# Convolutional linear attention and softmax attention in one kernel: tap copies on two queues, key taps between token products, and a last layer that works on pairs of images

## The chip, the cores and the metric

The kernel runs on one core of one Trainium2 chip. The metric is device time in microseconds (us), the median of several executions. TensorE multiplies, ScalarE and VectorE evacuate PSUM and do element-wise work, GpSimd does element-wise work in SBUF, and SyncE issues transfers; GpSimd and ScalarE issue some too.

## The reference

The input x is 4 images of 128 channels and 16 x 16 pixels, float32. The first layer is multi-scale linear attention:

```python
qkv = _conv(x, w_qkv)                      # 1x1, 384 channels
agg = _conv(_conv(qkv, w_dw, groups=384, pad=2), w_pw, groups=48)
qkv = concat([qkv, agg], axis=1)           # 32 heads of 24 channels: q, k, v of 8
q, k = relu(q), relu(k); v = pad(v, ones)
vk = einsum('bhdn,bhen->bhde', v, k)
out = einsum('bhde,bhen->bhdn', vk, q)
x = x + _conv(out[:, :, :-1] / (out[:, :, -1:] + EPS), w_proj)
```

The second layer is softmax attention over the 256 pixels of each image, with two 64-channel projections:

```python
t, p = W_theta @ x + b_theta, W_phi @ x + b_phi      # 64 x 256 per image
f = softmax(einsum('ndq,ndk->nqk', t, p) / 8, axis=-1)
x = x + W_fuse @ einsum('nqk,nck->ncq', f, x) + b_fuse
```

## The kernel before, in words

Every engine has a program written out by hand, in order; semaphores join them. There is no scheduler and no planner, so the order of the code is the order of the work.

**Opening.** SyncE loads the weights, then the depthwise 5 x 5 taps into tap_base (4 transfers, L303). The convolution works on pixels split into four phases, so a tap table shifted by a phase is needed on 128 partitions. For K this is done by TensorE: key_taps (L665) multiplies tap_base by a selection matrix. For Q and V it is done by transfers: SyncE waits for the taps and copies tap_base to tap_all sixteen times, 8 partitions each, for 4 phases and 4 quads (L316, semaphore taps_copied). VectorE's kept_taps (L491) multiplies taps by a mask, six operations for each kind, into wsel; wsel times the pointwise weights wpw_t gives wconv, by VectorE for K (L514) and by GpSimd for Q and V (L350, L355).

**Tokens, planes, convolution.** by_pixel (L671) makes the tokens of K, Q or V for one pair of images: four products, evacuated by ScalarE for pair 0 and by ScalarE or VectorE for pair 1 (L378, L475). to_planes (L682) transposes them, in the order pair 0, pair 1, pair 0, pair 1 in each half; ScalarE and VectorE copy these planes (L382, L479). convolve (L691) runs 144 products of 32 x 32 tiles for each kind, in three or four pieces with other work between them. The convolution of Q waits for wconv of Q, for the planes of Q, and for both evacuations of the convolution of K (L386, L532). Ahead of it stand plain_queries (L699) and some transposes of weights.

**Middle.** Key sums, denominators (L719), value-key products (L729), reciprocals and projections follow, all with TensorE as the engine that sets the pace.

**Last layer.** project(b, 1) (L859) finishes the first layer for image b in bank FIRST[b]; VectorE's first_layer (L606) adds xs into x1. Then for each image theta_phi_values makes in one bank, SECOND[b], the 128 rows of theta and phi (L885, 256 columns) and the values times W_fuse (L887, twice 128 columns). ScalarE evacuates theta and phi apart, 64 partitions each (L432, L434), into halves of tiles that hold two images. scores(pair) (L896) needs thetas and phis of both images of the pair, and uses each half of the array's rows for one image. VectorE takes the maxima (L610), ScalarE the exponentials with their sums (L445, two for each image), VectorE normalizes (L620, L623), TensorE transposes (L908), ScalarE evacuates for images 0, 2 and 3 (L451) and VectorE for image 1 (L627). attend (L916) gives the result, and VectorE adds bias and x1 (L633), which SyncE stores.

The order of the last layer is a list of steps for each engine; TensorE's is

```python
for step, b in ((theta_phi_values, 0), (theta_phi_values, 1), (theta_phi_values, 2), (scores, 0),
                (theta_phi_values, 3), (scores, 1), (transpose_probs, 0),
                (transpose_probs, 1), (attend, 0), (transpose_probs, 2), (attend, 1),
                (transpose_probs, 3), (attend, 2), (attend, 3)):
```

## Time and profile before

| what | value |
|---|---|
| median of 3 runs | 75.73 us (75.58 to 78.31) |
| the profiled execution | 75.22 us |
| its span, first to last instruction | 73.4 us |
| busy in the span: PE, VectorE, ScalarE, GpSimd | 63.9, 37.9, 24.5, 16.2 us |
| granted TensorE clock, mean | 1.00 |
| last ys written, end of the span | 71.3, 73.4 us |

Times of the trace are counted from the start of the span. The span lacks 1.8 us of the profiled execution's time. PE is TensorE's matmuls and PEld its weight loads; a float32 product appears as two records, a transpose as one. An idle time is put down to what ended it, in square brackets.

### The profile page before, as it was taken

How to read it: one execution, taken by the hardware profiler on the slowest of the kernel's cores; microseconds unless marked ns; L12 is line 12 of the kernel's file. 1: busy time of each engine (PE TensorE's matmuls, PEld its weight loads, DVE VectorE, ACT ScalarE, POOL GpSimd, SP SyncE). 2: the span in 40 equal slices, each digit the busy share in tenths (PEclk: the TensorE clock that was granted, in tenths of full speed). 3: DMA queues.
4: the chain of work that ended last, by engine and by line, in shares of the span. 5: the costliest groups of instructions: out<-in, count | busy, mean ns of one | idle time of the engine just before them, and what ended most of it. 6: DMA issues, size and time to landing. Idle time of an engine off the chain costs nothing.

```text
span 73.4 us, 2866 instructions
## 1 busy us (share of the span) xinstructions
PE 63.9 (87%) x1297; PEld 46.0 (63%) x1297; DVE 37.9 (52%) x96; ACT 24.5 (33%) x57; POOL 16.2 (22%) x22
## 2 busy tenths in 40 slices
PE   3999958999999699999999999999899591839960
PEld 3669846777867267466655766569589470628750
DVE  4540193002998547435049079595383037299660
ACT  0742460020317403005303000550203949688500
POOL 4307910000779999700000000000000000000000
PEclk9999999999999999999999999999999999999999
DMA  0863400002100000000000000000000000000143
GB/s 0 268 129 108 116 17 16 20 16 54 29 9 9 0 0 9 0 9 0 13 0 9 0 9 0 9 0 0 0 0 9 0 0 0 4 0 0 50 136 101
DMA packets 3484, 2.11 MB, mean 29 GB/s; under 512 B 1360, under 2 KB 3424, under 8 KB 3472
## 3 DMA queue, kind: packets, MB, share of 16 engines
q1 hardware_dynamic: 2672, 1.19, 6.0%
q10 hardware_dynamic: 544, 0.52, 2.1%
q0 software_dynamic: 256, 0.21, 1.2%
q8 instruction: 10, 0.16, 0.9%
q14 instruction: 2, 0.02, 0.1%
HBM read 1.24 MB, written 0.52 MB: 24 GB/s over the span
## 4 chain that ended last, share of the span: by engine, by line
PE 51%; SPq 15%; DVE 14%; DMA 7%; ACT 6%; issue 3%; ACTq 0%
PE bank L691 18%; SPq L316 13%; PE bank L916 5%; DMA tap_base<-in_L_conv_w_dw 4%; PE bank L859 4%; DVE wsel L491 4%; PE bank L896 3%; PE bank L739 3%; PE bank L729 3%; PE bank L705 3%; DMA tap_all<-tap_base 3%; PE bank L831 2%; PE bank L908 2%; ACT phi L434 2%; ACT theta L432 2%
## 5 line engine op out<-in xcount | busy, mean ns | idle before, releaser
L691 PE MATMUL bank<-planes,wconv 32*32 32x256 f32 x864 | 19.9, 397 | 1.7 <-DVE wconv L514 1.0
L691 PEld LDWEIGHTS bank<-planes,wconv 32*32 32x32 f32 x864 | 11.6, 103 | 8.3 <-issue 3.4
L671 PEld LDWEIGHTS bank<-wqkv_t,xp 128*128 128x128 f32 x48 | 6.5, 216 | 1.1 <-issue 0.9
L671 PE MATMUL bank<-wqkv_t,xp 128*128 128x128 f32 x48 | 6.8, 302 | 0.0
L491 DVE TENSOR_TENSOR wsel<-tap_all,consts 128x24 f32<-128x24 f32 x12 | 3.1, 327 | 6.3 <-DMA tap_all<-tap_base 6.3
L610 DVE TENSOR_REDUCE nmx<-bank 128x2 f32<-128x512 f32 x4 | 2.7, 687 | 5.5 <-PE bank L896 5.5
L378 ACT ACTIVATE toks<-bank 128x512 f32<-128x512 f32 x4 | 2.4, 597 | 9.0 <-PE bank L671 9.0
L649 PE MATMUL bank<-warm 128*128 128x256 f32 x8 | 4.0, 654 | 1.2 <-DVE warm L460 1.2
L896 PE MATMUL bank<-phi,theta 64*128 64x256 f32 x16 | 2.3, 402 | 2.5 <-ACT phi L434 2.5
L859 PE MATMUL bank<-qs,m 128*128 128x256 f32 x16 | 4.4, 402 | 0.0
L386 ACT ACTIVATE conv<-bank 128x512 f32<-128x512 f32 x3 | 1.8, 598 | 7.8 <-PE bank L691 7.8
L445 ACT ACTIVATE pr<-bank,nmx 128x256 f32<-128x256 f32 x8 | 3.7, 475 | 1.9 <-DVE nmx L610 1.8
L916 PE MATMUL bank<-pt,gf 128*128 128x256 f32 (+1 forms) x20 | 4.3, 352 | 0.0
L350 POOL TENSOR_TENSOR wconv<-wsel,wpw_t 128x1152 f32<-128x1152 f32 x1 | 2.2, 2175 | 9.3 <-DVE wsel L491 9.3
L554 DVE TENSOR_TENSOR vk<-bank,consts 64x128 f32<-64x128 f32 x8 | 2.3, 289 | 3.0 <-PE bank L729 2.9
L382 ACT ACTIVATE planes<-bank 128x512 f32<-128x512 f32 x4 | 2.4, 640 | 4.1 <-PE bank L682 4.1
L908 PE MATMUL bank<-ident,pn 128*128 128x128 f32 x16 | 2.5, 279 | 1.2 <-DVE pn L623 1.2
L562 DVE RECIPROCAL rden<-den 128x256 f32<-128x256 f32 x2 | 3.5, 1754 | 0.1
L649 PEld LDWEIGHTS bank<-warm 128*128 128x128 f32 x8 | 2.4, 333 | 1.5 <-DVE warm L460 1.2
L916 PEld LDWEIGHTS bank<-pt,gf 128*128 128x128 f32 x20 | 3.0, 190 | 0.6 <-ACT pt L451 0.2
L896 PEld LDWEIGHTS bank<-phi,theta 64*128 64x128 f32 x16 | 1.4, 186 | 3.0 <-ACT phi L434 2.9
L859 PEld LDWEIGHTS bank<-qs,m 128*128 128x128 f32 x16 | 2.7, 189 | 0.8 <-DVE qs L566 0.3
(107 smaller groups left out, 102.8 us busy)
## 6 DMA issues: line engine op xcount, KB each, us to landing
xs<-in_x ACTq DMA_DIRECT2D x2, 256.0 KB, 3.4
out<-ys SPq DMA_DIRECT2D x3, 128.0 KB, 1.7
tap_all<-tap_base SPq DMA_DIRECT2D x16, 9.6 KB
wqkv_n<-in_L_conv_w_qkv SPq DMA_DIRECT2D x3, 64.0 KB, 2.8
consts<-in_shape_constants POOLq DMA_DIRECT2D x1, 184.0 KB, 2.7
wproj_n<-in_L_conv_w_proj SPq DMA_DIRECT2D x1, 128.0 KB, 2.3
out<-ys SPq DMA_DIRECT2D x2, 64.0 KB, 1.6
tap_base<-in_L_conv_w_dw SPq DMA_DIRECT2D x4, 9.4 KB
```

The costliest lines, as they stand in the source:

```text
L316: sp.dma_start(dst, src).then_inc(taps_copied, 16)
L445: nc.scalar.activation(pr[:, b, qc, :], bank[:, FIRST[b], qc * N:(qc + 1) * N], ACT.Exp, bias=nmx[:, b, qc:qc + 1], accum_out=rs[:, b, qc: ...
L491: last = nc.vector.tensor_tensor(sel, src, mask, ALU.mult)
L562: nc.vector.reciprocal(rden[a][:, :], den[a][:, :]).then_inc(rden_out[a], 1)
L610: nc.vector.tensor_reduce(nmx[:, b, :], bank[:, FIRST[b], :].rearrange("p (q n) -> p q n", q=2), AX_X, ALU.max, negate=True).then_inc(nmx_ ...
L649: nc.tensor.matmul(bank[:, WARM, 0:N], warm[:, 0:P], warm[:, :], start=True, stop=True)
L671: last = nc.tensor.matmul(bank[:, TOK[kind][pair], a * P:(a + 1) * P], xp[:, pair, a, :], wqkv_t[:, kind, :], start=True, stop=True)
L691: last = nc.tensor.matmul(bank[32 * quad:32 * (quad + 1), i, 0:NPIX], w, window(i, kind, quad, n // WIN, n % WIN), start=n == 0, stop=n == ...
L859: last = nc.tensor.matmul(bank[:, FIRST[b], 0:N], m2[a][:, b, :], qs[:, b, a, :], start=a == 0, stop=a == 1)
L896: last = nc.tensor.matmul(bank[:, FIRST[2 * pair + n], qc * N:(qc + 1) * N], theta[rows, pair, qc * P:(qc + 1) * P], phi[rows, pair, :], s ...
L908: last = nc.tensor.transpose(bank[:, SECOND[b], at:at + P], pn[:, b, qc, kc * P:(kc + 1) * P], ident[:, :])
L916: last = nc.tensor.matmul(dst, gf[:, b, kc, :], pt[:, b, kc, pixels], start=kc == 0, stop=kc == 1)
```

## The change

**Tap copies.** SyncE issues those of phases 0 and 1, GpSimd those of phases 2 and 3, behind wpw_r and ahead of its constants and biases, with waits of its own for tap_base. VectorE waits for both semaphores ahead of wsel of Q and of V.

**Key taps.** TensorE does key_taps between the two token products of K, no longer behind them.

**Last layer.** thetas_phis(pair) makes the theta of both images of a pair in one bank, image 0 in the array's lower and image 1 in its upper 64 columns, and phi in another. ScalarE evacuates theta of a pair in one instruction of 128 partitions, VectorE phi in one. The values of a pair come later, together in one bank (the one that theta of the pair had), and are evacuated by one instruction of 512 columns on ScalarE. ScalarE evacuates all four images' transposed probabilities. The orders of all three engines are new. The step thetas_phis(0) stands ahead of project(3, 1).

```diff
+        THETA, PHI, GF, PT, REST = (2, 0), (3, 1), (2, 0), (3, 1, 2, 0), 3
...
+        def shifted_taps(a, i):
+
+            shift = TAPS * (a // 2) + a % 2
+            return (tap_all[32 * i + E * a:32 * i + E * (a + 1), :],
+                    tap_base[E * i:E * (i + 1), shift:shift + TAP_LEN + TAP_PAD])
...
-            for a in range(PHASES):
-                shift = TAPS * (a // 2) + a % 2
+            for a in range(PHASES // 2):
                 for i in range(QUADS):
-                    src = tap_base[E * i:E * (i + 1), shift:shift + TAP_LEN + TAP_PAD]
-                    dst = tap_all[32 * i + E * a:32 * i + E * (a + 1), :]
-                    sp.dma_start(dst, src).then_inc(taps_copied, 16)
+                    sp.dma_start(*shifted_taps(a, i)).then_inc(taps_copied, 16)
...
+            pool.wait_ge(base_zero, 2)
+            pool.wait_ge(ld_taps, 16 * QUADS)
+            for a in range(PHASES // 2, PHASES):
+                for i in range(QUADS):
+                    pool.dma_start(*shifted_taps(a, i)).then_inc(taps_moved, 16)
...
+            def thetas(pair):
+                act.wait_ge(theta_mm, pair + 1)
+                nc.scalar.activation(theta[:, pair, :], bank[:, THETA[pair], 0:N], ACT.Identity, bias=bth_s[:, 0:1],
+                                     scale=D ** -0.5).then_inc(theta_out, 1)
+
+            def values(pair):
+                act.wait_ge(gf_mm, pair + 1)
+                nc.scalar.activation(gf[:, 2 * pair:2 * pair + 2].rearrange("p b k c -> p (b k c)"), bank[:, GF[pair], :],
+                                     ACT.Copy).then_inc(gf_out, 1)
...
-                    dve.wait_ge(taps_copied, 16 * PHASES * QUADS)
+                    dve.wait_ge(taps_copied, 8 * PHASES * QUADS)
+                    dve.wait_ge(taps_moved, 8 * PHASES * QUADS)
...
+            def phis(pair):
+                dve.wait_ge(phi_mm, pair + 1)
+                nc.vector.tensor_scalar_add(phi[:, pair, :], bank[:, PHI[pair], 0:N], bph[:, 0:1]).then_inc(phi_out, 1)
...
+            for step, n in ((first_layer, 0), (first_layer, 1), (first_layer, 2), (phis, 0), (first_layer, 3), (maxima, 0),
+                            (phis, 1), (maxima, 1), (normalize, 0), (maxima, 2), (normalize, 1), (maxima, 3),
+                            (normalize, 2), (normalize, 3), (result, 0), (result, 1), (result, 2), (result, 3)):
+                step(n)
...
             by_pixel(K, 0)
-            pe.wait_ge(xp_act[1], 1)
-            pe.wait_ge(xp_dve[1], 1)
-            by_pixel(K, 1)
             pe.wait_ge(sel_set, 1)
             pe.wait_ge(base_zero, 2)
             pe.wait_ge(ld_taps, 16 * QUADS)
             key_taps()
+            pe.wait_ge(xp_act[1], 1)
+            pe.wait_ge(xp_dve[1], 1)
+            by_pixel(K, 1)
...
+            def thetas_phis(pair):
+
+                pe.wait_ge(x1_out, 2 * pair + 2)
+                for cols, i, done in ((slice(0, D), THETA[pair], theta_mm), (slice(D, 2 * D), PHI[pair], phi_mm)):
+                    for n in range(2):
+                        last = nc.tensor.matmul(bank[D * n:D * (n + 1), i, 0:N], wtp_t[:, cols], x1[:, 2 * pair + n, :],
+                                                start=True, stop=True)
+                    last.then_inc(done, 1)
+
+            def values(pair):
+                pe.wait_ge(theta_out, pair + 1)
+                for n in range(2):
+                    for kc in range(2):
+                        at = n * N + kc * C
+                        last = nc.tensor.matmul(bank[:, GF[pair], at:at + C], x1[:, 2 * pair + n, kc * P:(kc + 1) * P],
+                                                wfuse_t[:, :], start=True, stop=True)
+                last.then_inc(gf_mm, 1)
 
             def scores(pair):
-                pe.wait_ge(tp_out, 4 * pair + 4)
+                pe.wait_ge(theta_out, pair + 1)
+                pe.wait_ge(phi_out, pair + 1)
...
-                pe.wait_ge(gf_out[b], 1)
+                if b >= 2:
+                    pe.wait_ge(gf_out, b - 1)
...
-                pe.wait_ge(pt_out[b], 1)
+                pe.wait_ge(pt_out, b + 1)
+                pe.wait_ge(gf_out, b // 2 + 1)
...
+            project(2, 1)
+            thetas_phis(0)
+            project(3, 1)
+            scores(0)
+            thetas_phis(1)
+            values(0)
+            scores(1)
+            values(1)
+            transpose_probs(0)
+            transpose_probs(1)
+            attend(0)
+            transpose_probs(2)
+            attend(1)
+            transpose_probs(3)
+            attend(2)
+            attend(3)
 
```

TensorE in the opening, where xp are the pixels of x, tap_base the taps and toks the tokens; before:

```order
L671 MATMUL bank<-wqkv_t,xp 128x128 x8
L665 MATMUL bank<-tap_base,tap_sel 128x124 x4
L768 MATMUL bank<-ident,wpw_r 128x96
L682 MATMUL bank<-ident,toks 128x128 x8
L657 MATMUL bank<-ident,wqkv_n 128x128 x2
```

and of the change:

```order
L672 MATMUL bank<-wqkv_t,xp 128x128 x4
L666 MATMUL bank<-tap_base,tap_sel 128x124 x4
L672 MATMUL bank<-wqkv_t,xp 128x128 x4
L769 MATMUL bank<-ident,wpw_r 128x96
L683 MATMUL bank<-ident,toks 128x128 x8
```

The four products of taps (L665, now L666) stand four products earlier, and the second pair of K's tokens behind them.

TensorE at the start of the last layer, from the projections (qs, m) on; before:

```order
L859 MATMUL bank<-qs,m 128x256 x4
L885 MATMUL bank<-x,wtp_t 128x256
L887 MATMUL bank<-wfuse_t,x 128x128 x2
L885 MATMUL bank<-x,wtp_t 128x256
L887 MATMUL bank<-wfuse_t,x 128x128 x2
L885 MATMUL bank<-x,wtp_t 128x256
L887 MATMUL bank<-wfuse_t,x 128x128 x2
L896 MATMUL bank<-phi,theta 128x256 x4
L885 MATMUL bank<-x,wtp_t 128x256
L887 MATMUL bank<-wfuse_t,x 128x128 x2
L896 MATMUL bank<-phi,theta 128x256 x4
```

and of the change:

```order
L860 MATMUL bank<-qs,m 128x256 x3
L882 MATMUL bank<-x,wtp_t 64x256 x4
L860 MATMUL bank<-qs,m 128x256
L901 MATMUL bank<-phi,theta 128x256 x4
L882 MATMUL bank<-x,wtp_t 64x256 x4
L891 MATMUL bank<-wfuse_t,x 128x128 x4
L901 MATMUL bank<-phi,theta 128x256 x4
L891 MATMUL bank<-wfuse_t,x 128x128 x4
```

The products of x1 with wtp_t (theta and phi) are now of 64 columns and stand ahead of a projection and behind the first scores (phi, theta); those with wfuse_t (values) stand behind or between the scores.

ScalarE from the first theta on; before:

```order
L432 ACTIVATE theta<-bank,bth_s 64x256
L434 ACTIVATE phi<-bank,bph 64x256
L439 ACTIVATE gf<-bank 128x256
L432 ACTIVATE theta<-bank,bth_s 64x256
L434 ACTIVATE phi<-bank,bph 64x256
L432 ACTIVATE theta<-bank,bth_s 64x256
L434 ACTIVATE phi<-bank,bph 64x256
L445 ACTIVATE pr,rs<-bank,nmx 128x256 x2
L432 ACTIVATE theta<-bank,bth_s 64x256
L434 ACTIVATE phi<-bank,bph 64x256
L445 ACTIVATE pr,rs<-bank,nmx 128x256 x4
L451 ACTIVATE pt<-bank 128x512
```

and of the change:

```order
L440 ACTIVATE theta<-bank,bth_s 128x256 x2
L451 ACTIVATE pr,rs<-bank,nmx 128x256 x2
L445 ACTIVATE gf<-bank 128x512
L451 ACTIVATE pr,rs<-bank,nmx 128x256 x2
L445 ACTIVATE gf<-bank 128x512
L451 ACTIVATE pr,rs<-bank,nmx 128x256 x2
L457 ACTIVATE pt<-bank 128x512
L451 ACTIVATE pr,rs<-bank,nmx 128x256 x2
L457 ACTIVATE pt<-bank 128x512 x3
```

Phi is gone from ScalarE, each remaining theta and gf is of a pair, and four of pt stand there where there were three.

## Rows read from the trace of the kernel before

**Rows 1.** The page, chain that ended last, shares of the span by line

```profile
PE bank L691 18%; SPq L316 13%; PE bank L916 5%; DMA tap_base<-in_L_conv_w_dw 4%; PE bank L859 4%; DVE wsel L491 4%; PE bank L896 3%; PE bank L739 3%; PE bank L729 3%; PE bank L705 3%; DMA tap_all<-tap_base 3%; PE bank L831 2%; PE bank L908 2%; ACT phi L434 2%; ACT theta L432 2%
```

**Rows 2.** Tile tap_all: duration in ns min/median/max, first and last start

```profile
L316 SPq DMA_DIRECT2D tap_all<-tap_base x16: 624/625/753, 5.9 to 16.1; - x16
L491 DVE TENSOR_TENSOR wsel<-tap_all,consts x12: 172/175/1858, 17.9 to 21.4; 128x24 f32<-128x24 f32 x12
```

**Rows 3.** Chain in order of time: start, us, what

```profile
16.08 1.84 DMA tap_all<-tap_base
```

**Rows 4.** Timeline, opening: start, us, engine, line, operation, count, idle before

```profile
5.10 2.74 PE L671 MATMUL bank<-wqkv_t,xp 128*128 128x128 f32 x16
...
6.29 0.55 POOL L341 DMA_DIRECT2D consts<-in_shape_constants  x1
...
6.98 0.60 ACT L378 ACTIVATE toks<-bank 128x512 f32<-128x512 f32 x1 [1.44 <-PE bank L671]
...
7.76 1.15 PE L665 MATMUL bank<-tap_base,tap_sel 32*128 32x124 f32 x8
...
7.87 0.60 ACT L378 ACTIVATE toks<-bank 128x512 f32<-128x512 f32 x1 [0.29 <-PE bank L671]
...
8.99 1.04 PE L682 MATMUL bank<-ident,toks 128*128 128x128 f32 x8
...
9.69 1.16 ACT L382 ACTIVATE planes<-bank 128x512 f32<-128x512 f32 x2 [1.23 <-PE bank L682]
...
9.85 1.36 DVE L514 TENSOR_TENSOR wconv<-wsel,wpw_t 128x1152 f32<-128x1152 f32 x1
...
11.26 2.20 PE L691 MATMUL bank<-planes,wconv 32*32 32x256 f32 x96 [1.02 <-DVE wconv L514]
```

**Rows 5.** The page, transfers: KB each, median us from issue to landing

```profile
bth<-in_L_conv_b_theta POOLq DMA_DIRECT2D x2, 0.2 KB, 2.2
```

**Rows 6.** Timeline, 17 to 26 us, ahead of the convolution of Q

```profile
17.51 2.05 PE L671 MATMUL bank<-wqkv_t,xp 128*128 128x128 f32 x16
...
18.76 2.17 POOL L350 TENSOR_TENSOR wconv<-wsel,wpw_t 128x1152 f32<-128x1152 f32 x1 [9.31 <-DVE wsel L491]
...
22.18 1.41 DVE L527 MEMSET vk<- 64x256 f32 x4
...
23.24 1.13 PE L699 MATMUL bank<-xs,wqkv_t 128*128 128x512 f32 x2
...
23.63 0.69 DVE L532 TENSOR_SCALAR conv<-bank 128x512 f32<-128x512 f32 x1
...
25.06 2.20 PE L691 MATMUL bank<-planes,wconv 32*32 32x256 f32 x96 [0.70 <-DVE planes L479]
```

**Rows 7.** Timeline, denominators (L719) and the last layer

```profile
36.94 0.64 PE L719 MATMUL bank<-rq,ks 128*32 128x256 f32 x8
...
53.99 1.72 DVE L606 TENSOR_TENSOR x<-bank,xs 128x256 f32<-128x256 f32 x4
...
56.25 0.47 ACT L432 ACTIVATE theta<-bank,bth_s 64x256 f32<-64x256 f32 x1 [3.04 <-PE bank L887]
...
58.66 1.13 PE L896 MATMUL bank<-phi,theta 64*128 64x256 f32 x8 [0.78 <-ACT phi L434]
...
59.73 0.70 PE L885 MATMUL bank<-x,wtp_t 128*128 128x256 f32 x2
...
62.61 1.13 PE L896 MATMUL bank<-phi,theta 64*128 64x256 f32 x8 [1.75 <-ACT phi L434]
...
64.50 0.47 ACT L445 ACTIVATE pr<-bank,nmx 128x256 f32<-128x256 f32 x1 [0.90 <-DVE nmx L610]
...
65.42 0.60 ACT L451 ACTIVATE pt<-bank 128x512 f32<-128x512 f32 x1
...
67.50 1.13 PE L916 MATMUL bank<-pt,gf 128*128 128x256 f32 x4
...
69.97 1.33 DVE L633 SCALAR_TENSOR_TENSOR ys<-bank,bfu,x 128x256 f32<-128x256 f32 x3 [0.82 <-PE bank L916]
```

**Rows 8.** Busy us of each engine from 60 to 66, granted clock, transfers

```profile
60.00:66.00 6.00, 3.01 (x22) 2.15 (x21) 4.08 (x11) 4.47 (x16) 0.00 (x0) 1.00 0.00 1
```

More of the change, by code:

```diff
@@ L426, in _ @@
             act.wait_ge(bias_scaled, 1)
-            def theta_phi(b):
-                act.wait_ge(tf_mm, b + 1)
-                src = bank[:, SECOND[b], :]
-                rows = slice(D * (b % 2), D * (b % 2 + 1))
-                nc.scalar.activation(theta[rows, b // 2, :], src[0:D, 0:N], ACT.Identity, bias=bth_s[rows, 0:1],
-                                     scale=D ** -0.5).then_inc(tp_out, 1)
-                nc.scalar.activation(phi[rows, b // 2, :], src[D:2 * D, 0:N], ACT.Identity,
-                                     bias=bph[rows, 0:1]).then_inc(tp_out, 1)
-            def values(b):
-                act.wait_ge(tf_mm, b + 1)
-                nc.scalar.activation(gf[:, b].rearrange("p k c -> p (k c)"), bank[:, SECOND[b], N:2 * N],
-                                     ACT.Copy).then_inc(gf_out[b], 1)
+            def thetas(pair):
[6 more added lines that the diff above has]
+                                     ACT.Copy).then_inc(gf_out, 1)
             def exponentials(b):
@@ L450, in transposed @@
                 act.wait_ge(pt_mm, b + 1)
-                nc.scalar.activation(pt[:, b].rearrange("p k n -> p (k n)"), bank[:, SECOND[b], :], ACT.Copy).then_inc(pt_out[b], 1)
-            for step, b in ((theta_phi, 0), (values, 0), (theta_phi, 1), (theta_phi, 2), (exponentials, 0),
-                            (theta_phi, 3), (exponentials, 1), (exponentials, 2), (transposed, 0), (values, 2),
-                            (exponentials, 3), (values, 3), (transposed, 2), (transposed, 3)):
-                step(b)
+                nc.scalar.activation(pt[:, b].rearrange("p k n -> p (k n)"), bank[:, PT[b], :], ACT.Copy).then_inc(pt_out, 1)
+            for step, n in ((thetas, 0), (thetas, 1), (exponentials, 0), (values, 0), (exponentials, 1), (values, 1),
+                            (exponentials, 2), (transposed, 0), (exponentials, 3), (transposed, 1), (transposed, 2),
+                            (transposed, 3)):
+                step(n)
         @block.vector
@@ L637, in _ @@
             nc.vector.tensor_scalar_mul(bth_s[:, :], bth[:, :], D ** -0.5).then_inc(bias_scaled, 1)
[L638 to L642 removed]
+            for step, n in ((first_layer, 0), (first_layer, 1), (first_layer, 2), (phis, 0), (first_layer, 3), (maxima, 0),
+                            (phis, 1), (maxima, 1), (normalize, 0), (maxima, 2), (normalize, 1), (maxima, 3),
+                            (normalize, 2), (normalize, 3), (result, 0), (result, 1), (result, 2), (result, 3)):
+                step(n)
         @block.tensor
@@ L917, in attend @@
                     last.then_inc(y_mm, 1)
-            for step, b in ((theta_phi_values, 0), (theta_phi_values, 1), (theta_phi_values, 2), (scores, 0),
-                            (theta_phi_values, 3), (scores, 1), (transpose_probs, 0),
-                            (transpose_probs, 1), (attend, 0), (transpose_probs, 2), (attend, 1),
-                            (transpose_probs, 3), (attend, 2), (attend, 3)):
-                step(b)
+            pe.wait_ge(m2_act[1], 1)
+            project(0, 1)
+            project(1, 1)
+            pe.wait_ge(m2_dve, 1)
+            project(2, 1)
[14 more added lines that the diff above has]
+            attend(3)
 _INS = ["x", "L0_conv_w_qkv", "L0_conv_w_dw", "L0_conv_w_pw", "L0_conv_w_proj", "L1_conv_W_theta",
```

40 lines of the change are left out of this document (8 added, 32 removed).

## The prediction

> **What bounds the kernel now.** I read the chain that ended last by line first, then the chain in order of time, then the timeline of its two weak places, the opening and the last layer. The chain is mostly TensorE, but its second largest line is no work at all: SyncE's issues of the tap copies, 13% [rows 1]. The reader is to see sixteen issues of 0.62 us one behind the other, first start 5.9, last start 16.1 [rows 2], and behind them a landing of 1.84 us that ends at 17.92 [rows 3]. Only then, at 17.9, can VectorE make wsel of Q [rows 2]. The share of 13% is not what can be won, though: TensorE works on through all of this, and what it loses is read from its own idle time, 0.70 us ahead of the convolution of Q at 25.06 [rows 6]. So the tap copies are worth 0.7 us, not 10. Nearly everything between 25 and 53 us is TensorE without a pause, and I move it as one block. The third place is the last layer: there TensorE stands idle twice ahead of the scores (L896), 0.78 and 1.75 us, each time for a phi that ScalarE evacuates [rows 7]. Between 60 and 66 us it is busy for only 3.01 of 6 us [rows 8]. That is the large loss.
>
> **Key taps between the token products.** TensorE does not wait for anything up to 7.8 us, so only the order changes. Sixteen records of L671 take 2.74 us from 5.10, and the clock they run at is lower in the first half: ScalarE could start on pair 0 at 6.98 and on pair 1 at 7.87 [rows 4]. The taps (1.15 us) come at about 6.9 and are done at 8.0, 0.9 us earlier than before (7.76 + 1.15 = 8.91). VectorE's wsel of K goes with them, but what follows it, wpw_t, waits for a transpose that TensorE issues at 8.85 as before; I let wpw_t start at 9.2, behind that transpose; its quarter of a microsecond brings wconv of K to 9.5 instead of 9.85, so that its 1.36 ends about 0.35 earlier, near 10.85 [rows 4]. Against that, the second pair of K's tokens is now done at 8.8 instead of 7.85. ScalarE's 0.60 for it ends at 9.4, and the transposes to planes, which from the second one on need both pairs, cannot go before. Before, planes started 0.70 behind the first transpose (8.99 to 9.69); now three of the four transposes of that half are left at 9.45, 2 steps of 0.11 and 0.27 to the end of the last, and planes start at 9.98. Its 1.16 ends at 11.1, and the first convolution starts at 11.2 instead of 11.26. I take 0.05 gained, so nothing: the wait for wconv has become a wait for planes. The bounds are 0.35 gained (planes not late) and 0.75 lost, which is next.
>
> **Taps on two queues.** SyncE issues 8 instead of 16 copies: 5.89 + 8 x 0.66 = 11.2, and with 1.84 they land at 13.0 [rows 2, 3]. GpSimd issues the other 8 from 6.33 (behind wpw_r, and its new waits for tap_base, which landed at 5.8). No row shows a GpSimd issue of this shape; the nearest are 0.55 for a large constant and 2.2 us of landing for a small bias [rows 4, 5]: 6.33 + 8 x 0.55 + 2.2 = 12.9. So both halves are there at 13.0, 4.9 us sooner. Behind them on GpSimd's queue stand the constants and five bias loads, each moved by 4.4 us, to about 13.9, then wconv of Q. The constants are wanted at 33, the biases at 54. SyncE's three last-layer weights are issued 5.3 us earlier and nobody waits for them.
>
> What VectorE makes of it: wsel of Q runs at 13.0 to 13.7, the Q tokens as TensorE delivers them near 15.5, wsel of V directly after, the V tokens at 19.6 (TensorE's 17.51 + 2.05), the zero fills (1.41) until about 21.7 [rows 6]. At 21.7 the convolution of K is done, and its evacuation starts at once instead of at 23.63; the Q planes are ready by 23.5. TensorE's last work ahead of the convolution of Q, plain_queries, ends at 24.37 (23.24 + 1.13). It starts there: **0.70 us gained**, and not more, since TensorE's own work ends last. GpSimd's wconv of Q (2.17) is done at about 16.1, long before. One stall goes with it and gives nothing more: one of the twelve wsel operations took 1.86 us where the median is 0.175 [rows 2], beside GpSimd's wconv of 18.76 to 20.9 [rows 6]. Now wsel of V starts only when that wconv is over.
>
> That row is also the danger. It reads as if VectorE's first wsel of V was held until GpSimd's multiplication was over, so that the two exclude each other for some operations. The Trainium skill (SBUF — State Buffer, "SBUF: two separate sides") says that VectorE in some modes and GpSimd share a port pair by an exclusive lock, and that the descriptors of GpSimd's DMAs are written through it. The trace agrees for the multiplication, by the 1.86 us; for DMA issues no row shows it. In this kernel it would be wconv of K on VectorE, at 9.5, beside the last two issues of taps and those of the constants. At worst the two issues that are left at 9.5 hold it, 2 x 0.55 = 1.1 us; 0.35 of that is cover, so 0.75 lost at the first convolution, and the 0.70 is gone. I take zero: what held VectorE was a multiplication over whole tiles, and a DMA issue is not that.
>
> **The last layer.** I lay it out in the times of before, to be moved by 0.70 as a whole. Removed: eight evacuations of 64 partitions by ScalarE (0.47 each, 3.8 us), replaced by two thetas on ScalarE and two phis on VectorE. Four values of 256 columns become two of 512. All four transposed probabilities now go to ScalarE, which loses VectorE's help there (0.6 more). Step by step [rows 7]:
> - x1 of image 1 is there at 53.99 + 2 x 0.43 = 54.85. The theta and phi products of the pair use 64 columns of the array each. No row has that tile. The nearest are L719, four tiles of 32 columns, whose 8 records take 0.64 us, that is side by side, and L896, two tiles of 64 rows, 8 records in 1.13. If they don't overlap, 8 records cost 8 x 0.22 = 1.7 instead of 0.9. I take L896's 1.13: phi is ready at 56.0, VectorE's 0.43 ends at 56.45, scores start at 56.5 (before: 58.66).
> - Projection 3 is tucked between; x1 of image 3 comes at 56.9 instead of 55.7, still ahead of its use.
> - TensorE is free 1.07 after the scores start (58.66 to 59.73): 57.6 [rows 7]. Then theta and phi of pair 1 (0.96), values 0 (eight records of 0.11 and 0.1 for the switch, 1.0), scores 1 (1.0), values 1 (its results 1.15 after its start): 58.55, 59.55, 60.5, 61.65. Without a wait, since theta 1 is ready at 58.8, phi 1 at 59.1.
> - ScalarE: exponentials 0 and 1 fit before 61.65. From there on: values 1 0.60, exponentials 2 0.92 (64.50 to 65.42), transposed 0 0.60, exponentials 3 0.92, transposed 1 0.60, with 0.05 at the seams: 65.4. Attend 1 starts there, before it was at 67.50. TensorE has done attend 0 and the transposes of image 2 meanwhile (63.9 to 65.2).
> - From attend 1 to the end the work is the same: 67.50 to the end of the last ys, 71.30, is 3.80. Image 3's probabilities are normalized at 65.7, transposed at 66.3. **2.1 us gained.**
>
> Each switch between whole array and halves costs 0.1 in my sum: four rounds of L896, 0.22 apart (two records of L885 take 0.70, one 0.48), are 0.88, and the next product came after 1.07; I give half of the 0.19 to the start behind a wait and half to the switch. I have six switches on the path. The Trainium skill (TensorEngine Tiling (Array Packing), "Tiling Modes", Key Properties) says that changing the mode drains TensorE. By a full drain L885 could not have started before L896's last end, 59.79, where it started at 59.73: 0.06 more for each switch, 0.4 for six, and 1.7 gained in place of 2.1. The row decides for me.
>
> **Sum.** 0.70 + 2.1 = 2.8 off the profiled execution's 75.22: 72.4. The median of the runs, 75.73, lies 0.5 above that execution; but I counted every evacuation of ScalarE at its full length, with no overlap at the seams. I say 72.5.
>
> **Rivals.**
> 1. The 64-column products don't overlap. Then 0.87 more twice, 1.7: 74.2. For it: no row has the tile. Against it: L719.
> 2. The opening gives nothing, because GpSimd's issues hold VectorE's wconv of K: 75.22 - 2.1 = 73.1, or 73.2 with the offset. For it: the 2.47 row. Against: its cover of 0.35.
> 3. ScalarE binds the last layer. From theta 1 (58.3) to transposed 1 it has nine steps: 0.47 + 4 x 0.92 + 4 x 0.60 = 6.55, to 64.9, which is 0.5 short of binding. If exponentials take 1.05 and each step pays 0.1 at its seam, that is 66.3 and attend 1 is 0.9 late: 73.3, and 73.7 with full drains. For it: it inherits all four transposed probabilities. Against it: it loses half of its theta and phi work.
> 4. Slower: the clock falls in the last layer. Up to 6.8 us L671's records came at 0.215, later products of that size at 0.11, so half speed doubles them. If it fell behind the scores 0, the chain would hold 4.1 us (57.6 to 61.65) and 3.1 (attend 1 to the end) of TensorE's work: 72.4 + 7.2 = 79.6. It decides from 2.8 us of such work on the chain (4.3 for slower by 2%). Against it: the granted clock stayed at 1.00 between 60 and 66 us with pauses up to 1.75 [rows 8], and the longest new pause in my layout is 1.4, ahead of attend 0.
>
> **Chances.** Forecast 0.62 (its own range 71.3 to 73.3); rival 1 0.10; rival 2 0.11; rival 3 0.07; rivals 1 and 2 together, 74.9, 0.07; rival 4 0.03. About 2% is what a measurement of this kernel can tell from no change, so faster means under 74.2. The forecast, rivals 2 and 3 and half of rival 1 are under it: 0.85; the rest of 1, and 1 with 2, is the same: 0.12; slower 0.03. Range 71.3 (planes not late, switches free: 0.35 and 0.5 more) to 74.2.
>
> **What would show it.** Right: no issue of taps in the chain; wsel of Q near 13; the convolution of Q 0.7 us earlier, without an idle wait; theta and phi records in pairs with the same start; scores near 55.8 and attend 1 near 64.7. Wrong: wconv of K on VectorE over 1.4 us; records of L882 spread 0.22 apart without pairs; ScalarE waiting over 0.5 us ahead of an exponential; a last granted clock under 1.00.

## The result, and the profile after

The changed kernel takes 72.53 us (median of 4 runs, 72.38 to 72.72); the kernel before, run beside it, takes 76.87 (median of 4, 75.58 to 78.31). Runs in a slower state, like the 78.00 and 78.31 of the kernel before, are left out of all ratios. The ratio is 0.963, interval 0.960 to 0.966. The forecast was 72.5 in a range of 71.3 to 74.2. The profiled execution took 72.72 for the 75.22 of before, its span 70.6 for 73.4: 2.8 us less in the span and 2.5 in all. In two profiles below the granted clock is 0.50 for a while (both opening edits alone, from 62.7 to 69.5 us, and the new last layer alone, from 25.5 to 28.9), and only their other stages are read.

The page of the changed kernel, the chain that ended last by engine and by line; it answers to [rows 1]:

```profile
PE 86%; ACT 5%; DVE 4%; issue 1%; ACTq 0%
PE bank L692 27%; PE bank L672 9%; PE bank L923 6%; PE bank L650 5%; PE bank L683 4%; PE bank L860 3%; PE bank L740 3%; PE bank L730 3%; PE bank L901 3%; PE bank L891 3%; PE bank L700 3%; PE bank L882 3%; PE bank L706 3%; PE bank L832 2%; DVE vk L561 2%; ACT planes L392 2%
```

SyncE's issues, 13% before, are gone from the chain. What took their place is TensorE's own work in the opening (L672, L683, the warm-up products L650), which had been there all the time beside them. That is why 13% of the chain were worth only 1% of the time.

The timeline of the changed kernel's opening, columns as in [rows 4]; it answers to [rows 4] and [rows 6]:

```profile
5.18 1.26 PE L672 MATMUL bank<-wqkv_t,xp 128*128 128x128 f32 x8
6.03 5.47 SPq L321 DMA_DIRECT2D tap_all<-tap_base  x8
6.37 1.15 PE L666 MATMUL bank<-tap_base,tap_sel 32*128 32x124 f32 x8
6.76 4.05 POOL L350 DMA_DIRECT2D tap_all<-tap_base  x8 [0.28 <-issue]
7.45 1.16 PE L672 MATMUL bank<-wqkv_t,xp 128*128 128x128 f32 x8
8.65 0.60 ACT L388 ACTIVATE toks<-bank 128x512 f32<-128x512 f32 x1 [1.57 <-PE bank L672]
9.10 1.36 DVE L521 TENSOR_TENSOR wconv<-wsel,wpw_t 128x1152 f32<-128x1152 f32 x1
9.30 0.98 PE L683 MATMUL bank<-ident,toks 128*128 128x128 f32 x7 [0.49 <-ACT toks L388]
9.95 1.16 ACT L392 ACTIVATE planes<-bank 128x512 f32<-128x512 f32 x2 [0.70 <-PE bank L683]
11.25 2.20 PE L692 MATMUL bank<-planes,wconv 32*32 32x256 f32 x96 [0.75 <-ACT planes L392]
...
13.61 0.65 DVE L498 TENSOR_TENSOR wsel<-tap_all,consts 128x24 f32<-128x24 f32 x6 [2.58 <-DMA tap_all<-tap_base]
14.43 2.17 POOL L360 TENSOR_TENSOR wconv<-wsel,wpw_t 128x1152 f32<-128x1152 f32 x1 [0.43 <-DVE wsel L498]
...
16.14 1.10 DVE L498 TENSOR_TENSOR wsel<-tap_all,consts 128x24 f32<-128x24 f32 x6
...
24.28 1.70 PEld L692 LDWEIGHTS bank<-planes,wconv 32*32 32x32 f32 x96 [0.76 <-issue]
24.28 2.10 PE L692 MATMUL bank<-planes,wconv 32*32 32x256 f32 x90
```

The reader is to see: the taps arrive at 13.6 instead of 17.9; the convolution of Q starts at 24.28 instead of 25.06 and PE waits for no engine ahead of it; the first convolution starts where it did (11.25 for 11.26), but what ended its wait is now the planes, not wconv, which was ready at 10.46. And the first eight records of token products take 1.26 us, where the sixteen of [rows 4] took 2.74: the clock rose earlier in this execution. That will matter below.

The last layer of the changed kernel; it answers to [rows 7]:

```profile
54.11 1.08 PE L882 MATMUL bank<-x,wtp_t 128*64 128x256 f32 x8
54.89 0.47 ACT L440 ACTIVATE theta<-bank,bth_s 128x256 f32<-128x256 f32 x1 [2.48 <-PE bank L882]
55.12 0.30 PEld L860 LDWEIGHTS bank<-qs,m 128*128 128x128 f32 x2 [0.39 <-issue]
55.12 0.70 PE L860 MATMUL bank<-qs,m 128*128 128x256 f32 x2
55.24 0.48 DVE L622 TENSOR_SCALAR phi<-bank,bph 128x256 f32<-128x256 f32 x1 [0.75 <-PE bank L882]
...
55.87 1.14 PE L901 MATMUL bank<-phi,theta 64*128 64x256 f32 x8
...
61.30 0.60 ACT L445 ACTIVATE gf<-bank 128x512 f32<-128x512 f32 x1 [0.64 <-PE bank L891]
...
61.79 0.47 ACT L451 ACTIVATE pr<-bank,nmx 128x256 f32<-128x256 f32 x1
...
62.69 0.60 ACT L457 ACTIVATE pt<-bank 128x512 f32<-128x512 f32 x1
...
63.17 0.49 ACT L451 ACTIVATE pr<-bank,nmx 128x256 f32<-128x256 f32 x1
...
63.35 1.13 PE L923 MATMUL bank<-pt,gf 128*128 128x256 f32 x4 [1.02 <-ACT pt L457]
...
64.75 1.13 PE L923 MATMUL bank<-pt,gf 128*128 128x256 f32 x4
...
67.22 1.33 DVE L635 SCALAR_TENSOR_TENSOR ys<-bank,bfu,x 128x256 f32<-128x256 f32 x3 [0.82 <-PE bank L923]
```

Attend 1 starts at 64.75 for 67.50 before, and the last ys ends at 68.55 for 71.30: 2.75 us, of which 0.78 came in with the convolution of Q. The stretch of 60 to 66 us, to be held against [rows 8]:

```profile
60.00:66.00 6.00, 4.98 (x33) 4.05 (x32) 4.01 (x13) 4.66 (x16) 0.00 (x0) 1.00 0.00 0
```

TensorE is busy for 4.98 of the 6 us where it was for 3.01, at the same granted clock.

### The profile page after: what moved, and what is told of

It is laid out like the page before. It is cut to its first block, busy times and chain, and to the rows that moved or that the text cites. A ratio compares the mean times of both kernels' runs of the same rounds, so it can differ in the third digit from the quotient of the medians.

```text
span 70.6 us, 2883 instructions
## 1 busy us (share of the span) xinstructions
PE 64.2 (91%) x1305; PEld 44.8 (63%) x1305; DVE 37.0 (52%) x96; ACT 22.1 (31%) x51; POOL 20.4 (29%) x30
## 4 chain that ended last, share of the span: by engine, by line
PE 86%; ACT 5%; DVE 4%; issue 1%; ACTq 0%
PE bank L692 27%; PE bank L672 9%; PE bank L923 6%; PE bank L650 5%; PE bank L683 4%; PE bank L860 3%; PE bank L740 3%; PE bank L730 3%; PE bank L901 3%; PE bank L891 3%; PE bank L700 3%; PE bank L882 3%; PE bank L706 3%; PE bank L832 2%; DVE vk L561 2%; ACT planes L392 2%
## 5 line engine op out<-in xcount | busy, mean ns | idle before, releaser
L672 PEld LDWEIGHTS bank<-wqkv_t,xp 128*128 128x128 f32 x48 | 6.0, 199 | 1.2 <-issue 0.9
L672 PE MATMUL bank<-wqkv_t,xp 128*128 128x128 f32 x48 | 6.5, 287 | 0.0
L650 PE MATMUL bank<-warm 128*128 128x256 f32 x8 | 4.0, 654 | 1.2 <-DVE warm L466 1.2
L350 POOL DMA_DIRECT2D tap_all<-tap_base x8 | 4.1, 514 | 0.3 <-issue 0.3
L683 PE MATMUL bank<-ident,toks 128*128 128x128 f32 x24 | 3.4, 280 | 0.5 <-ACT toks L388 0.5
L683 PEld LDWEIGHTS bank<-ident,toks 128*128 128x128 f32 x24 | 2.6, 141 | 1.6 <-issue 0.9
L650 PEld LDWEIGHTS bank<-warm 128*128 128x128 f32 x8 | 2.4, 333 | 1.5 <-DVE warm L466 1.2
L481 DVE COPY toks<-bank 128x512 f32<-128x512 f32 x2 | 1.4, 692 | 3.6 <-PE bank L672 3.6
L485 DVE COPY planes<-bank 128x512 f32<-128x512 f32 x2 | 1.4, 692 | 3.3 <-PE bank L683 3.3
```

Of the source, the lines that this page charges most:

```text
L350: pool.dma_start(*shifted_taps(a, i)).then_inc(taps_moved, 16)
L650: nc.tensor.matmul(bank[:, WARM, 0:N], warm[:, 0:P], warm[:, :], start=True, stop=True)
L672: last = nc.tensor.matmul(bank[:, TOK[kind][pair], a * P:(a + 1) * P], xp[:, pair, a, :], wqkv_t[:, kind, :], start=True, stop=True)
L683: last = nc.tensor.transpose(bank[:, PLANE[kind][half], n * P:(n + 1) * P], src, ident[:, :])
```

## The experiments

Eleven kernels were run and the changed one a second time. Since medians of one kernel differ by more than some of the parts (last experiment), I read each part from its stage in the profile, and give the ratio to the kernel before beside it. All the stage lengths are differences of starts in the timelines:

| kernel | slow steps | first token product to first convolution | first convolution to that of Q | last projections to last ys | ratio to before (interval) |
|---|---|---|---|---|---|
| before | 8 | 6.16 | 13.80 | 18.04 | |
| changed | 2 | 6.07 | 13.03 | 16.09 | 0.963 (0.960 to 0.966) |
| tap copies on two queues alone | 0 | 5.38 | 13.04 | 18.04 | 0.983 (0.977 to 0.990) |
| key taps moved alone | 1 | 6.20 | 14.26 | 18.04 | 0.999 (0.996 to 1.003) |
| both opening edits | 1 | 5.97 | 13.10 | (clock) | none |
| last layer alone | 0 | 5.38 | 14.81 | 16.08 | 0.974 (0.968 to 0.980) |
| same half | 0 | 5.96 | 13.04 | 17.79 | none |
| projection first | 0 | 6.01 | 13.04 | 16.37 | 0.974 (0.968 to 0.980) |
| values later | 4 | 6.31 | 13.04 | 15.21 | 0.956 (0.949 to 0.964) |
| VectorE helps | 1 | 5.95 | 13.05 | 15.99 | 0.970 (0.959 to 0.981) |
| key taps in old place | 7 | 6.05 | 13.04 | 16.09 | 0.959 (0.952 to 0.965) |
| best | 2 | 5.56 | 13.03 | 15.21 | 0.954 (0.950 to 0.958) |
| taps last on GpSimd | 7 | 6.86 | 13.03 | 16.09 | 0.971 (0.968 to 0.973) |
| changed, again | 4 | 6.27 | 13.03 | 16.08 | 0.970 (0.965 to 0.974) |

"Slow steps" counts, of the sixteen records of K's first token products, those that follow the one ahead by more than 0.16 us (most of them by 0.21) and not by 0.11. I take them for the time that the clock stayed at its lower level (1.2 of 2.4 GHz). The profile's clock column reads 1.00 in this stretch too, but the trace's first entry of a full clock stands at 6.7 us in the kernel before and at 5.6 in the changed one, where the steps become short; and from 66 to 69 us of the profile of both opening edits, where the granted clock is 0.50, records of 128 columns come at the same 0.21. One step of 0.21 is not counted: the second record behind the taps has it in every kernel with the new order, also at 7.67 us of the changed one, long after the clock has risen. "Last projections" is the first product of project(0, 1).

**Tap copies on two queues alone.** The edit is the part of the change on SyncE, GpSimd and VectorE's wait, in the kernel before.

> The kernel before, with only the tap copies on two queues. My theory: TensorE's idle time of 0.70 us ahead of the convolution of Q goes, and nothing else in the opening counts: 0.7 to 0.8 us less than the kernel before, near 74.8 by medians. The rival, that the opening's gain needs the key taps' new place too (the first convolution earlier), gives less than 0.4. The rival that GpSimd's issues hold VectorE's wconv of K shows wconv of K over 1.4 us and gives nothing.

```profile
10.41 2.20 PE L700 MATMUL bank<-planes,wconv 32*32 32x256 f32 x96 [1.02 <-DVE wconv L523]
...
23.45 2.20 PE L700 MATMUL bank<-planes,wconv 32*32 32x256 f32 x96
```

Its timeline: the convolution of Q comes 13.04 after the first, for 13.80 before, and its own idle note is gone: 0.76 us, all of the idle time and no more. The first convolution is early too, at 10.41; the edit has no part in that, since its reason is the 0 slow steps, and the new last layer alone, whose opening is that of before, has 0 slow steps and the same 5.38. GpSimd's issues did not hold wconv of K. My theory holds for the stage, and its number. By time the kernel is 1.3 us below the one before (74.20 for 75.51 by medians), more than I expected; in the profile the early first convolution is 0.85 of it.

**Key taps moved alone.**

```diff
             by_pixel(K, 0)
-            pe.wait_ge(xp_act[1], 1)
-            pe.wait_ge(xp_dve[1], 1)
-            by_pixel(K, 1)
...
             key_taps()
+            pe.wait_ge(xp_act[1], 1)
+            pe.wait_ge(xp_dve[1], 1)
+            by_pixel(K, 1)
```

> The kernel before, with only the key taps moved between the two token products of K. My theory: wconv of K is ready 0.35 us earlier, but the planes of K come later than it, so the first convolution starts within 0.15 of 11.26 and the time is the same within 0.2 us. The rival, that the planes are not late, starts it at 10.9; then TensorE waits longer ahead of the convolution of Q instead, since the tap copies still land at 17.9, and the time is the same as well, so the start of the first convolution tells them apart, not the time.

Its timeline, TensorE in the opening:

```profile
4.77 1.16 PE L671 MATMUL bank<-wqkv_t,xp 128*128 128x128 f32 x8
6.13 1.12 PE L665 MATMUL bank<-tap_base,tap_sel 32*128 32x124 f32 x8 [0.20 <-DMA tap_base<-in_L_conv_w_dw]
7.18 1.16 PE L671 MATMUL bank<-wqkv_t,xp 128*128 128x128 f32 x8
...
9.03 0.98 PE L682 MATMUL bank<-ident,toks 128*128 128x128 f32 x7 [0.49 <-ACT toks L378]
...
10.97 0.84 PE L691 MATMUL bank<-planes,wconv 32*32 32x256 f32 x33 [0.75 <-ACT planes L382]
```

The time is the same, as both theories said, because the taps of Q still land late: the 14.26 us to the convolution of Q swallow whatever happens ahead. The start of the first convolution, 10.97, is nearer to the rival's 10.9 than to mine. But the comparison with 11.26 was wrong, for both: that number belongs to a profile with 8 slow steps, this one has 1. Counted from the first token product, the old order takes 5.38 with no slow step and 5.56 with 2 (best, below), and this one takes 6.20. So it is neither theory: the move costs time. The rows say how. The first convolution waits for planes, the planes for the transposes, these for the second pair of tokens, and that now stands behind 1.1 us of taps and, when the clock is early, behind a wait of 0.20 for tap_base as well.

**Both opening edits, old last layer.**

> The kernel before, with both edits of the opening and the old last layer. My theory: 0.75 us less than before, the same as the tap copies on two queues alone within 0.15. The rival, that the two edits help each other: 1.0 us or more less than before.

No ratio can be given: its four runs took 74.10 to 76.84 us, two of them at a mean granted clock of 0.955 and 0.954. Its opening gives 13.10 to the convolution of Q and 5.97 to the first: what the two edits do alone, and no help of one to the other that the rival wanted. Inconclusive as to time.

**Last layer alone.** The changed kernel with both opening edits undone.

> The changed kernel with both edits of the opening undone. My theory: the parts add up, so the last layer alone gives 1.95 us less than before (the trace of the changed kernel has attend 1 at 64.75 for 67.50, of which 0.8 is the opening's). The rival, that the new last layer only gains because it starts earlier or that some of it is lost with the opening: under 1.6 or over 2.4 us.

16.08 us from the last projections to the last ys, for 18.04 before and 16.09 in the changed kernel. The new last layer is worth 1.96 us with either opening, so the parts add; the ratio 0.974 is 1.9 us by 75.

**Same half.** The 64-column products put where they can't lie side by side. Image 1's theta and phi are then written over image 0's, so the result is wrong and only the time counts:

```diff
-                        last = nc.tensor.matmul(bank[D * n:D * (n + 1), i, 0:N], wtp_t[:, cols], x1[:, 2 * pair + n, :],
+                        last = nc.tensor.matmul(bank[0:D, i, 0:N], wtp_t[:, cols], x1[:, 2 * pair + n, :],
```

> The changed kernel, with theta and phi of both images of a pair written to the lower 64 columns of the array and the same 64 partitions, so that they can't lie side by side. It leaves the upper image's theta and phi out of the result. My theory: the 8 records of each pair take about 1.9 us instead of 1.08, both pairs on the chain, so the time is 1.5 to 1.8 us above the changed kernel (near 74.2 by medians). The rival, that ScalarE's row of exponentials binds and TensorE has slack there, gives under 0.9 us more.

Its timeline, TensorE, both pairs of theta and phi:

```profile
54.04 1.94 PE L882 MATMUL bank<-x,wtp_t 128*64 128x256 f32 x8
...
57.72 1.94 PE L882 MATMUL bank<-x,wtp_t 128*64 128x256 f32 x8
```

1.94 for 1.08, twice, and the stage is 1.70 us longer (17.79 for 16.09), which is rival 1's price. Its runs took 73.70 to 75.07 us, for the 72.38 to 72.72 of the changed kernel. So the two halves do overlap in the changed kernel, and TensorE's products up to the values are on the chain without slack.

**Projection first.** project(3, 1) ahead of thetas_phis(0), as before:

```diff
-            thetas_phis(0)
             project(3, 1)
+            thetas_phis(0)
```

> The changed kernel with project(3, 1) ahead of thetas_phis(0), as the old order had it. It takes away one change of the array's mode, and it fills TensorE's wait for x1 of image 1. My theory: phi of pair 0 comes some 0.05 to 0.2 us later, x1 of image 3 a whole microsecond earlier, VectorE has x1 of image 3 ahead of phi: 0 to 0.2 us slower, or the same. The rival, that switches of mode are dear: 0.2 us faster or more.

0.28 us slower in its stage, a little over what I expected. Its timeline has the scores waiting for phi:

```profile
54.51 1.08 PE L882 MATMUL bank<-x,wtp_t 128*64 128x256 f32 x8
56.27 1.13 PE L901 MATMUL bank<-phi,theta 64*128 64x256 f32 x8 [0.68 <-DVE phi L622]
```

The projection fills the time in which phi is evacuated; it is worth more there than one switch of the array costs.

**Values later.** One list, ScalarE's:

```diff
-            for step, n in ((thetas, 0), (thetas, 1), (exponentials, 0), (values, 0), (exponentials, 1), (values, 1),
-                            (exponentials, 2), (transposed, 0), (exponentials, 3), (transposed, 1), (transposed, 2),
+            for step, n in ((thetas, 0), (thetas, 1), (exponentials, 0), (values, 0), (exponentials, 1), (exponentials, 2),
+                            (transposed, 0), (transposed, 1), (exponentials, 3), (values, 1), (transposed, 2),
```

> The changed kernel with another order on ScalarE alone: exponentials 2 and both first transposed probabilities ahead of exponentials 3, and values 1 behind those. In the changed kernel ScalarE waits 0.64 us for values 1 at 61.30 and TensorE then 1.02 us for transposed 0 at 63.35. My theory, that ScalarE's order is what sets attend 0 and 1: attend 0 about 0.8 us earlier, the end 0.6 to 1.0 us earlier. The rival, that TensorE's row of products behind it binds: under 0.3 us.

Its timeline, both attends:

```profile
63.23 1.13 PE L923 MATMUL bank<-pt,gf 128*128 128x256 f32 x4 [0.16 <-ACT pt L457]
...
64.63 1.03 PE L923 MATMUL bank<-pt,gf 128*128 128x256 f32 x4
```

TensorE's wait ahead of attend 0 falls from 1.02 to 0.16 us, and the stage from 16.09 to 15.21: 0.88 us, as expected. In the changed kernel ScalarE stands still for 0.64 us for values that nobody needs before attend 2, with exponentials 2 queued behind. The edit also puts transposed 1 ahead of exponentials 3; what each of the two moves gives is not separated.

**VectorE helps.** Image 1's transposed probabilities to VectorE again (its own semaphore, one entry from ScalarE's list to VectorE's).

> The changed kernel with VectorE evacuating the transposed probabilities of image 1, as before, ahead of its normalize 3. My theory: ScalarE is relieved of 0.5 us ahead of attend 1 and 2, but attend 1 starts at 64.75 directly behind TensorE's transposes of image 2, so it gains nothing, and VectorE's normalize 3 comes 0.6 later at most: the same within 0.2 us. The rival, that ScalarE binds by its sum: 0.4 us faster or more.

0.10 us faster in its stage; TensorE's wait ahead of attend 0 stays at 1.01. The sum of ScalarE's work is not the bound, its order is.

**Key taps in the old place, in the changed kernel; and best,** which is that and values later together.

> The changed kernel with the key taps back behind both token products of K. My theory, from the first convolution's start and the moment TensorE's clock rises in the runs so far: with the clock up at 4.9 us the old order starts the first convolution at 10.4 to 10.5 and the new one at 10.9 to 11.0, so the move costs 0.5 us, all of it on the chain now that the taps are not late. The first convolution starts at 10.4 to 10.5 and the time is 0.4 to 0.5 us below the changed kernel. The rival, that the difference came from the clock alone and the move is worth nothing or something: at the same clock the start is 10.9 or later, and the time is that of the changed kernel.

> Tap copies on two queues, key taps in their old place, the new last layer, and ScalarE's exponentials 2 ahead of values 1. My theory: the parts add. Against the changed kernel 0.5 us for the key taps and 0.88 us from the last projections to the last ys (15.2 instead of 16.1): near 71.2 by medians, 0.94 of the kernel before. The rival, that one eats the other: over 71.8.

The timeline of best, TensorE's opening products and first convolution:

```profile
5.28 2.13 PE L672 MATMUL bank<-wqkv_t,xp 128*128 128x128 f32 x16
...
10.84 2.20 PE L692 MATMUL bank<-planes,wconv 32*32 32x256 f32 x96 [1.02 <-DVE wconv L521]
```

In both, the clock rose later than I had counted on, so the starts of 10.4 to 10.5 did not come. Each slow step adds 0.10 us in either order: the old order has 5.38 with none, 5.56 with 2, 6.05 with 7 and 6.16 with 8, the new one 5.95 and 5.97 with 1, 6.07 with 2, 6.27 and 6.31 with 4. With 2 steps each the orders are 5.56 and 6.07. Taken step by step, what exceeds 0.11 leaves 5.38 for the old order in all five kernels and 5.87 for the new one in all nine (the waits for tap_base and the slow steps of the taps themselves taken off too). So the move costs 0.49 us at the first convolution, the 0.5 that I expected. With 7 steps, where the taps themselves began at the lower clock, the pair is 6.05 and 6.86. The median of key taps in the old place, 72.84 (71.80 to 72.96), does not show it, and by time alone that experiment is inconclusive. Best is at 71.76 us (71.45 to 72.27), 0.954 of before; its interval and the changed kernel's in the first comparison do not meet. I had expected 71.2, and the rival anything over 71.8, so the time nearly took the rival's side, while the stages, 5.56 and 15.21, are those of the parts. By its profile the first convolution starts 0.4 us later than I counted on (10.84 for 10.45): 0.18 are the slow steps, the rest is the first token product's start at 5.28. Another 0.2 is a stop in the middle, told in the last experiment.

**Taps last on GpSimd.** Its eight copies behind the constants and biases.

> The changed kernel with GpSimd's eight tap copies issued behind its constants and biases, some 3.2 us later, so that they land near 16.5 instead of 13.5. My theory, that only TensorE's 0.70 us of idle time were to be won and the landing has slack: wsel of Q near 16.7, the convolution of Q still starts 13.05 after the first one, same time within 0.2 us. The rival, that every microsecond of the copies counts: 1 us or more slower. In between: GpSimd's wconv of Q now lies against wsel of V on VectorE and holds it for up to 1.9 us, and if that is enough to make VectorE late, the convolution of Q starts 13.1 to 13.8 after the first.

```profile
16.34 0.66 DVE L498 TENSOR_TENSOR wsel<-tap_all,consts 128x24 f32<-128x24 f32 x6 [4.45 <-DMA tap_all<-tap_base]
17.15 2.17 POOL L360 TENSOR_TENSOR wconv<-wsel,wpw_t 128x1152 f32<-128x1152 f32 x1 [3.58 <-DVE wsel L498]
17.51 2.46 DVE L498 TENSOR_TENSOR wsel<-tap_all,consts 128x24 f32<-128x24 f32 x6
```

The copies are there 2.7 us later, GpSimd's wconv of Q holds VectorE's wsel of V again, and the convolution of Q still comes 13.03 after the first. The landing has that much slack, and my theory holds for the stage. The time, 72.94, is 0.4 above the first median of the changed kernel and 0.3 below its second; that can't be told from no change.

**The changed kernel again.**

> The changed kernel once more, unaltered, to see how much of the differences between the variants' medians is the variants'. My theory: the stages repeat to 0.1 us (13.03 from the first convolution to that of Q, 16.1 from the last projections to the last ys), while the start of the first convolution moves with the moment TensorE's clock rises, 0.4 us for each microsecond, and the value-key products are held by 0 to 0.5 us. Then the ratio to the kernel before comes out between 0.958 and 0.971. The rival, that runs on another chip differ in the stages themselves, shows another 13.03 or 16.1.

Its timeline in the middle, value-key products (L730):

```profile
40.75 1.03 PE L730 MATMUL bank<-kt,vt 64*64 64x64 f32 x50
41.94 0.45 PE L730 MATMUL bank<-kt,vt 64*64 64x64 f32 x14 [0.16 <-issue]
```

73.22 us (72.43 to 73.41) and 0.970, inside what I expected: the same kernel, 0.7 us above its first median. The stage to the convolution of Q and the last layer are the same to 0.01. What differs is the start of the first convolution (4 slow steps for 2, 11.42 for 11.25) and a stop behind the 50th of the 64 records of the first value-key products. It made the stretch up to the next product 0.48 us longer here. It was there in nine of the fourteen profiles, where that stretch was 0.20 to 0.85 us longer than in the kernel before, always behind the same record, and absent in five with the same code at that place. The profile names no engine for it, only "issue". The page of the profile has one more trace of it, its DMA queues:

```profile
q8 instruction: 10, 0.16, 0.9%
```

These are ten packets of 16 KB in the queue that the profile marks as instructions; for which engine, it does not say. In every profile one starts 1.1 to 1.8 us ahead of the value-key products. In the nine with the stop the 51st record starts 1.28 to 1.50 us after that packet's end; in the five without, the products get there by themselves 1.35 to 1.68 us after it. The stop is longest, 0.75 us between two records, where the packet ended last, 0.09 us after the first of the products had started (taps last on GpSimd). So the stop looks like a wait for instructions that came late. No experiment here moved the fetch, so this is argued and not shown.

## Why the prediction was right

The time was right to 0.03 us by the first median, and that is partly luck: the same kernel took 73.22 the second time, and errors cancelled twice. In the opening, what the key taps cost was given back by a clock that rose earlier than in the profile of before; in the last layer, a longer row of TensorE was made good by shorter steps of ScalarE. At the same clock the three parts give 0.76 - 0.49 + 1.96 = 2.2 us and not 2.8.

**Taps on two queues: right.** 0.70 forecast, 0.76 measured alone, and also the reason: TensorE's own work ends last. The landing was at 13.6, not 13.0: SyncE's issues began 0.14 later and took 0.68 each, and the last landed 2.7 us after its issue started, at 10.87. The 1.84 of before counts from the start of an issue too (16.08 to 17.92), and I had added it to the end. GpSimd's half was there at 11.95. The slack hid all this. GpSimd's issues took 0.50, not 0.55. The danger that I named did not come: wconv of K took its 1.36 us at 9.10 to 10.46, beside GpSimd's issues that ran on at 0.50 each.

One sentence of it was wrong: that wsel of V starts only when GpSimd's wconv is over. It took 1.10 us at 16.14, held until that wconv ended at 16.60. It cost nothing.

**Key taps: wrong.** I took "0.05 gained, so nothing". The step that failed is "the second pair of K's tokens is now done at 8.8". I had it start at 8.0 and gave its eight records 0.8 us; they take 1.16, also at full clock (7.45 to 8.61 in the changed kernel), because the first two records behind the taps come 0.09 and 0.10 us late. And at the clock of before, which I assumed, the taps are not done at 8.0: with 7 slow steps (taps last on GpSimd) the second pair was done 4.22 us after the first token product, which is 9.3 in the times of before. The planes and the first convolution went with it. The direction was seen (the wait for wconv has become a wait for planes), the size was not. The result hid it: the changed kernel's first convolution did start at 11.25, as I said, but with 2 slow steps where the kernel before had 8, and those are 0.6 us. At equal clock the move costs 0.49 us.

**Last layer: right in sum, 2.1 forecast and 1.96 measured, with two terms that cancel.** In the times of before (0.78 later), scores began at 56.65 (56.5 forecast), values 1 were ready at 62.1 (61.65): TensorE's row was 0.45 longer than forecast. It starts 0.15 late, since a phi evacuation takes 0.48 and not 0.43 and the scores start 0.15 behind its end and not 0.05; and its four steps behind the scores took 0.05 to 0.11 more each, 0.30 together, for which the switches (next paragraph) are enough. ScalarE then made it good: values to exponentials 0.49 and transposed to exponentials 0.48, where I had counted the full 0.60, and exponentials to transposed 0.90. Attend 1 at 65.53, for 65.4.

**The switches of the array.** I had read 0.1 us for a switch, and it is nearer 0.2. My working took two records of L885 that last 0.70 together and one that lasts 0.48 to be 0.22 apart; but the second lasts only 0.38, so they are 0.32 apart. In the changed kernel, from the 64-column records to the whole-array projection, the step is 0.31 us ahead of the first record of the new kind and 0.32 ahead of the second, where it is 0.21 to 0.22 without a switch; from the 64-column records to the values it is 0.31 and 0.21 for 0.21 and 0.11. That is 0.20 us for a switch; from the scores to 64 columns it was 0.14. The second part alone, 0.10, also follows a wait without a switch: the first two records of attend 0, at 63.35, are 0.32 apart. The Trainium skill (TensorEngine Tiling (Array Packing), "Tiling Modes") says that a switch drains TensorE. Here the whole-array projection starts at 55.12, 0.07 us before the end of the last 64-column record (54.11 + 1.08 = 55.19). The ends of these records are modelled, so 0.07 does not settle whether it drains; the steps between starts give the price.

**The port pair.** The Trainium skill (SBUF — State Buffer, "SBUF: two separate sides") has VectorE and GpSimd exclude each other on a shared port pair, for an operation of VectorE with two inputs in SBUF against one of GpSimd that reads SBUF. The rows agree three times for multiplications: wsel of V took 2.47, 1.10 and 2.46 us, each time until GpSimd's multiplication ended, and 0.65 without one beside it. For the descriptors of GpSimd's DMAs the same section names only VectorE's two-port modes, and wconv of K is a multiplication with two inputs. So my reading of it for rival 2 went too far; neither wconv of K nor the issues beside it were longer.

**The rivals.** Rival 1 was priced well (1.7 for 1.70) and did not happen. Rival 2 did not happen either: what threatened the opening was the order of TensorE, not a port. Rival 3 had the right engine and the wrong mechanism: ScalarE does not bind by its sum, it binds at one place by its order, 0.88 us that the changed kernel leaves lying. Rival 4 did not happen in the changed kernel; the granted clock was 1.00 from 60 to 66 us.

## What to carry to other kernels

A share of the chain of waits is not a gain: read what the next engine's idle time is at the place where the stages meet, and give an edit no more than that. When an instruction is moved ahead of another, add its duration to the other's chain and follow that chain to its end, even where the first chain gets shorter. In an in-order queue, look for the instruction that waits for something needed late with something needed early behind it; and compare stages, not medians, when the parts are smaller than the scatter of one kernel.

## What was not expected of the hardware

The moment at which TensorE's clock rises differs between executions of the same opening: 0 to 8 of the sixteen records of K's first token products came at 0.21 us steps, the rest at 0.11, and the first convolution follows by 5.38 to 6.16 us in the old order. Both ends of this range are of the same opening code, the new last layer alone and the kernel before. It is a lottery of 0.8 us in a kernel of 73. The stop behind the 50th record of the value-key products, none to 0.85 us, is another. Between the two profiles of the changed kernel they make 0.17 and 0.48 of the 0.7 us in the span.

The clock can also fall in mid-kernel. In 13 of the 44 runs of the kernel before that were made beside the experiments, the mean granted clock was 0.93 to 0.98, and they took 76.4 to 79.6 us for about 75.4. In none of the 43 runs of kernels with the tap copies on two queues and the new last layer was it below 0.99. Two profiles caught a fall, and in both TensorE had just stood idle: it was busy for 0.40 of the 2 us up to 62, ahead of the old last layer's second scores (fall at 62.7), and it waited 1.67 us until 25.29 for planes, ahead of the convolution of Q whose taps came late (fall at 25.5). The change takes both idle stretches away. Whether this is why the clock no longer fell, no run tests.
